# Adjacency masks made on GpSimd instead of VectorE, with one-byte edges moved in pairs, in a two-layer graph attention kernel

## The chip, the cores and the metric

The kernel runs on one core of a Trainium2 chip. Its time is the device time of one execution in microseconds. The core has five engines that run their own instruction streams and meet at semaphores: TensorE (PE, with its weight loads as PEld), VectorE (DVE), ScalarE (ACT), GpSimd (POOL) and SyncE (SP), which here only issues DMAs.

## What is computed

Two graph attention layers over 6144 nodes with 128 features, each with a residual and a layer norm. `adj` is a 6144 x 6144 matrix of int32 zeros and ones (151 MB), and both layers mask with it.

```python
def _L0_gnn_ref(xx_anchor, input, adj, weight):
    anchor_adj = jnp.einsum('md,de,ne->mn', xx_anchor, weight, input)
    scores = jnp.where(adj > 0, anchor_adj, NEG_PAD)
    return jax.nn.softmax(scores / TEMPERATURE, axis=1) @ input

def _L1_gnn_ref(mole_out, adj, W, a1, a2):
    Wh = mole_out @ W
    e = jax.nn.leaky_relu((Wh @ a1)[:, None] + (Wh @ a2)[None, :], negative_slope=0.2)
    att = jax.nn.softmax(jnp.where(adj > 0, e, NEG_INF), axis=1)
    return jax.nn.elu(att @ Wh)

x = _layernorm(x + _L0_gnn_ref(x, L0_gnn_input, adj, L0_gnn_weight), axis=-1)
x = _layernorm(x + _L1_gnn_ref(x, adj, L1_gnn_W, L1_gnn_a1, L1_gnn_a2), axis=-1)
```

## The kernel before

**Layer 0** takes 48 tiles of 128 rows (index t), each in 12 chunks (c) of 512 columns. For each chunk PE makes the scores in three f16 matmuls (lines 462 to 464). DVE adds the mask to them, takes the maximum and writes them to `rows` (L693). After the tile's last chunk DVE makes the bias of the exponential (L752, L756). One tile later ACT exponentiates (L589), PE transposes the result in f32 (L452), ACT copies its high half (L583), DVE makes the low half (L702), and PE multiplies both by `vals` (L428, L430). The end of a tile (scale, residual, layer norm: L720 to L747) is spread over the chunks 3 to 9 of DVE two tiles later. Its reciprocal root is made on POOL (L329), between L744 and L747 of DVE: L747, in chunk 9, waits for it.

**Masks and edges.** SP loads `adj` in four quarters q of 128 x 1536 int32 per tile into `adj_sb`, which holds one tile. DVE turns a quarter into a bf16 mask, 0 or -2^60 (`make_mask`, L670). POOL turns the mask into bf16 edges, 1 or 0 (`make_edges`, L314). SP stores the edges to `edge_rows` in HBM (L250). `neg_mask` and `edges` each hold one tile. So a quarter of the next tile's mask waits for three things: its `adj` has landed, DVE has used the old mask (`masked`), and POOL has turned it to edges (`edges_set`). SP loads a quarter of `adj` once the mask before it is made (`mask_set`, L259); ahead of a tile's loads it waits for PE's transposes L386 and L415 of earlier tiles (L255, L267).

**The first tile** also makes z and `vals`: DVE has z_low (L649), vals_low (L656) and L693 for each chunk, and POOL scales `vals` in four pieces (L306).

**Between the layers** PE makes Wh in 48 matmuls of one node block each (L494), copied out by ACT and DVE.

**Layer 1** takes 12 groups (g) of 512 rows. SP reads the edges back through the transposing DMA, eight parts of six node blocks per group, into four slots of `edgesT`, which lie over the masks (L282). DVE multiplies each of the 48 blocks of edges with the weights (L865, out in eight slots `p1`), and PE accumulates four products of it into PSUM (L523, each f32 matmul being two records in the trace). The group's end is spread over DVE and POOL (L346 to L368). `r_all` holds a factor per row of the group, spread over the partitions by PE (L501) and copied by ACT (L631).

The order of each engine's work is written out by hand: `tile_steps` of each engine and `tile_rstd` of POOL.

Of the kernel before, what the change touches and what calls it, by code (L numbers as in the profile page):

```python
# [31 lines left out]
def build(nc, x, adj, inp, w0, w1, a1, a2, edge_rows, out):  # L32
# [15 lines left out]
    with ExitStack() as ctx:  # L48
# [246 lines left out]
        def _(pool):  # L295
# [13 lines left out]

            def make_edges(t, q):  # L310

                after(pool, edges_out[q], 16 * t)
                pool.wait_ge(mask_set, QUARTERS * t + q + 1)
                nc.gpsimd.tensor_scalar(edges[:, q, :], neg_mask[:, q, :], 1.0 / MASK_BIG, 1.0, ALU.mult,  # L314
                                        ALU.add).then_inc(edges_set, 1)

            for q in range(QUARTERS // 2):
                make_edges(0, q)

            def tile_rstd(t, par, known):  # L320
                ahead = known is None or known < NB - 1
                if scores_of(known):
                    for q in range(QUARTERS // 2, QUARTERS):
                        make_edges(t, q)
# [565 lines left out]
```

## Time and profile before

| | us |
|---|---|
| median of 3 runs (1623.17 to 1624.73) | 1623.41 |
| the profiled execution | 1624.58 |
| its span, first to last instruction | 1622.8 |
| first tile's bias (L756) ends about | 52.9 |
| last tile's bias ends about | 1050.6 |
| first layer 1 weights (L865) start | 1084.8 |

The profiled execution is 1.2 us longer than the median. Layer 0 takes nearly two thirds of the span and layer 1 one third. Busy times are shares of the span, and a busy PE may be a PE whose matmuls wait in line behind each other, so the stages are read one by one. "Idle before, releaser" tells for how long an engine stood still before a line's instructions, and what let it go on.

### The profile page before, as it was taken

Reading aid. Unit: us, or ns where it says so; the run is one execution under the profiler, and the core shown is the slowest. Engines: PE = TensorE matmul, PEld = TensorE weight load, DVE = VectorE, ACT = ScalarE, POOL = GpSimd, SP = SyncE. Lnnn points to the kernel's source line nnn. Section 1 sums busy time; section 2 is a strip of 40 time slices with the busy share of each in tenths; the row PEclk is TensorE's granted clock in tenths of the full one; section 3 lists DMA queues with packets and bytes.
Section 4 is the critical chain, followed back from the end, with each engine's and each line's share of the span. In section 5 each row is a group of like instructions: output and inputs, shape, how many; then the busy total and the mean of one; then the engine's idle time right before and its main releaser. Section 6 shows DMA issues by size and latency. Waiting matters only on the chain.

```text
span 1622.8 us, 36456 instructions
## 1 busy us (share of the span) xinstructions
PE 1583.5 (98%) x13614; PEld 1331.7 (82%) x13614; DVE 1506.9 (93%) x3368; ACT 868.9 (54%) x2111; POOL 431.1 (27%) x330
## 2 busy tenths in 40 slices
PE   6799999999999999999999999989999999999996
PEld 3577777777777777777777777789999999999996
DVE  6999999999999999999999999978999999999996
ACT  3577777777777777777777777881000000000000
POOL 5322323333323232323333232200222222222120
PEclk9899999999999999999999999999999999999998
DMA  7756666666666666666666666447767777767781
GB/s 239 242 181 225 236 239 241 241 240 233 221 224 219 222 222 230 235 241 240 241 238 222 221 220 224 142 83 154 161 145 154 151 151 148 150 144 154 145 163 33
DMA packets 380398, 317.07 MB, mean 195 GB/s; under 512 B 306240, under 2 KB 331072, under 8 KB 380224
## 3 DMA queue, kind: packets, MB, share of 16 engines
q1 hardware_dynamic: 380224, 314.75, 63.6%
q8 instruction: 109, 1.79, 0.4%
q14 instruction: 65, 0.53, 0.1%
HBM read 160.56 MB, written 78.64 MB: 147 GB/s over the span
## 4 chain that ended last, share of the span: by engine, by line
PE 92%; issue 3%; DVE 2%; ACT 1%; POOL 0%; POOLq 0%; DVEq 0%; ACTq 0%
PE ps L523 29%; PE ps L452 15%; PE ps L428 15%; PE ps L430 8%; PE ps L464 7%; PE ps L463 7%; PE ps L462 7%; DVE adj_sb L865 1%; PE ps L494 0%; ACT rows L589 0%; PE ps L415 0%; PE ps L386 0%; ACT pT_hi L583 0%; PE ps L501 0%; PE ps L531 0%
## 5 line engine op out<-in xcount | busy, mean ns | idle before, releaser
L523 PE MATMUL ps<-rows,adj_sb 128*128 128x129 f32 x4608 | 516.7, 275 | 1.4 <-DVE adj_sb L865 1.4
L523 PEld LDWEIGHTS ps<-rows,adj_sb 128*128 128x128 f32 x4608 | 515.6, 192 | 1.6 <-issue 1.6
L865 DVE SCALAR_TENSOR_TENSOR adj_sb<-rows,late,edge_sb 128x512 f32<-128x512 f32 x576 | 440.2, 797 | 44.3 <-PE ps L523 21.2
L428 PE MATMUL ps<-vals,pT_hi 128*128 128x256 f16 x2304 | 442.5, 273 | 0.9 <-ACT att L577 0.8
L583 ACT CAST pT_hi<-ps 128x512 f16<-128x512 f32 x576 | 336.9, 585 | 192.0 <-PE ps L452 181.8
L589 ACT ACTIVATE rows<-rows,exp_bias 128x512 f32<-128x512 f32 x576 | 417.2, 724 | 19.8 <-DVE exp_bias L756 19.8
L693 DVE CUSTOM_DVE_ANT_0 rows<-ps,edge_sb 128x512 f32<-128x512 f32 x576 | 396.3, 688 | 26.0 <-PE ps L464 13.8
L430 PE MATMUL ps<-vals,pT_lo 128*128 128x128 f16 x2304 | 411.7, 219 | 0.0
L314 POOL TENSOR_SCALAR edge_sb<-edge_sb 128x1536 bf16<-128x1536 bf16 x192 | 283.0, 1474 | 470.4 <-DVE edge_sb L670 470.3
L702 DVE TENSOR_TENSOR pT_lo<-ps,pT_hi 128x512 f16<-128x512 f32 x576 | 394.9, 686 | 6.0 <-ACT pT_hi L583 5.8
L452 PE MATMUL ps<-ident,rows 128*128 128x128 f32 x2304 | 349.5, 274 | 2.8 <-DVE pT_lo L702 2.8
L428 PEld LDWEIGHTS ps<-vals,pT_hi 128*128 128x128 f16 x2304 | 225.7, 98 | 87.1 <-DVE pT_lo L702 1.3
L430 PEld LDWEIGHTS ps<-vals,pT_lo 128*128 128x128 f16 x2304 | 225.7, 98 | 66.3 <-issue 0.3
L452 PEld LDWEIGHTS ps<-ident,rows 128*128 128x128 f32 x2304 | 247.3, 141 | 10.1 <-issue 3.7
L628 ACT ACTIVATE zT<-ps,late 128x128 f32<-128x128 f32 x48 | 13.7, 368 | 434.7 <-DVE late L803 434.7
L462 PE MATMUL ps<-zT,xT_hi 128*128 128x512 f16 x576 | 219.4, 381 | 4.4 <-DVE vals L656 4.3
L463 PE MATMUL ps<-zT,xT_hi 128*128 128x512 f16 x576 | 219.3, 381 | 0.0
L464 PE MATMUL ps<-zT,xT_lo 128*128 128x512 f16 x576 | 219.3, 381 | 0.0
L670 DVE TENSOR_SCALAR edge_sb<-adj_sb 128x1536 bf16<-128x1536 int32 x192 | 185.6, 966 | 0.0
L464 PEld LDWEIGHTS ps<-zT,xT_lo 128*128 128x128 f16 x576 | 56.6, 98 | 68.6 <-issue 1.3
L589 ACT ACTIVATION_READ_ACCUMULATOR rows<-rows,exp_bias 128x1 f32 x576 | 109.9, 191 | 0.0
L329 POOL TENSOR_TENSOR small<-small,consts 128x1 f32<-128x1 f32 x48 | 26.4, 550 | 266.5 <-DVE small L744 266.5
(99 smaller groups left out, 737.1 us busy)
## 6 DMA issues: line engine op xcount, KB each, us to landing
adj_sb<-adj SPq DMA_DIRECT2D x192, 768.0 KB, 8.2
edge_rows<-edge_sb SPq DMA_DIRECT2D x192, 384.0 KB, 7.8
rows<-inp SPq DMA_DIRECT2D x4, 768.0 KB, 9.0
xq<-x SPq DMA_DIRECT2D x48, 64.0 KB, 2.0
xr<-x SPq DMA_DIRECT2D x48, 64.0 KB, 1.9
out<-vals SPq DMA_DIRECT2D x12, 256.0 KB, 2.6
edge_sb<-edge_rows SPq DMA_TRANSPOSE x96, 5.6
x1T<-w SPq DMA_DIRECT2D x1, 64.0 KB, 1.9
```

The source lines that it names most:

```text
L428: nc.tensor.matmul(acc, pT_hi[:, s, cols], vals[:, jb, :], start=(jb == 0), stop=False, skip_group_check=True)
L430: mm = nc.tensor.matmul(acc[:, P:2 * P], pT_lo[:, s, cols], vals[:, jb, 0:P], start=False, stop=(jb == NB - 1), skip_group_check=True)
L452: mm = nc.tensor.transpose(ps[:, PT0 + bc % NPT, b * P:(b + 1) * P], rows[:, pb * N + bc * CHUNK + b * P:pb * N + bc * CHUNK + (b + 1) * P ...
L462: nc.tensor.matmul(scores_bank(c), xT_hi[:, par, :], zT[:, 0, cols], start=True, stop=False)
L463: nc.tensor.matmul(scores_bank(c), xT_hi[:, par, :], zT[:, 1, cols], start=False, stop=False)
L464: nc.tensor.matmul(scores_bank(c), xT_lo[:, par, :], zT[:, 0, cols], start=False, stop=True).then_inc(scored, 1)
L523: mm = nc.tensor.matmul(ps[:, 4 * par + k, 0:P + 1], p1_slot(n)[:, k * P:(k + 1) * P], vals1[:, n, 0:P + 1], start=(n == 0), stop=(n == NB ...
L583: nc.scalar.copy(pT_hi[:, bc % PT_SLOTS, :], ps[:, PT0 + bc % NPT, :]).then_inc(pT_hi_set, 1)
L589: nc.scalar.activation(row_chunk(1 - par, c), row_chunk(1 - par, c), ACT.Exp, bias=exp_bias[:, 1 - par:2 - par], scale=EXP_SCALE, accum_ou ...
L693: nc.vector.tensor_tensor_reduce(row_chunk(par, c), scores_bank(c), neg_mask[:, c // QC, w:w + CHUNK], 1.0, -3.0e38, ALU.add, ALU.max, par ...
L702: nc.vector.tensor_tensor(pT_lo[:, s, :], ps[:, PT0 + bc % NPT, :], pT_hi[:, s, :], ALU.subtract).then_inc(pT_lo_set, 1)
L865: nc.vector.scalar_tensor_tensor(out=p1_slot(n), in0=r_all[:, bass.ds(g * CHUNK, CHUNK)], scalar=col_of[:, E_OF, n:n + 1], in1=edgesT[:, p ...
```

## The change

- `make_mask` moves from DVE to POOL, same operation and shape: int32 in, bf16 out. POOL makes mask and edges of a quarter one after the other. In a tile t it makes quarter 3 of this tile and quarters 0 and 1 of the next, then the reciprocal root, then quarter 2 of the next.
- In the first tile POOL makes a mask and its edges after each of the first three pieces of `vals`.
- Edges are kept as one byte each (`edges`, a buffer of its own) and stored as pairs in 16-bit words: half the bytes of each store and of each transposing DMA. `edgesT` gets its slots over the masks alone.
- A transposed pair holds two neighbouring nodes, so DVE reads `edgesT` as bytes with a step of two, and block jb of layer 1 is the even or the odd nodes of 256. The order of Wh's rows (`x1T_pairs`) and of `r_all` follows.

```diff
-        edge_sb = sb("edge_sb", [P, 2, QUARTERS, QW], BF16)
-        neg_mask = edge_sb[:, 0]
-        edges = edge_sb[:, 1]
+        edge_sb = sb("edge_sb", [P, PART_SLOTS * PB * CHUNK // 2], U16)
+        neg_mask = edge_sb[:, 0:N].bitcast(BF16).rearrange("p (q w) -> p q w", w=QW)
+        edges = sb("edges", [P, QUARTERS, QW // 2], U16)
+        edge_bytes = edges[:].bitcast(U8)
...
+        edgesT_bytes = edge_sb[:].bitcast(U8).rearrange("p (s b w h) -> p s b h w", b=PB // 2, w=CHUNK, h=2)
+        x1T_pairs = x1T[:].rearrange("d (u p h) -> d u h p", p=P, h=2)
...
-                sp.dma_start(edge_rows[bass.ds(t * P, P), q * QW:(q + 1) * QW], edges[:, q, :]).then_inc(edges_out[q], 16)
+                sp.dma_start(edge_rows[bass.ds(t * P, P), q * QW // 2:(q + 1) * QW // 2], edges[:, q, :]).then_inc(edges_out[q], 16)
...
+            def make_mask(t, q):
+                pool.wait_ge(adj_in[q], 16 * (t + 1))
+                after(pool, masked, C * (t - 1) + (q + 1) * QC if t > 0 else 0)
+                after(pool, edges_set, QUARTERS * (t - 1) + q + 1 if t > 0 else 0)
+                nc.gpsimd.tensor_scalar(neg_mask[:, q, :], adj_sb[:, q, :], 0.0, -MASK_BIG, ALU.is_le,
+                                        ALU.mult).then_inc(mask_set, 1)
+            def make_edges(t, q):
+                after(pool, edges_out[q], 16 * t)
+                pool.wait_ge(mask_set, QUARTERS * t + q + 1)
+                nc.gpsimd.tensor_scalar(edge_bytes[:, q, :], neg_mask[:, q, :], 1.0 / MASK_BIG, 1.0, ALU.mult,
+                                        ALU.add).then_inc(edges_set, 1)
...
+                if t < NB:
+                    make_mask(t, QUARTERS - 1)
+                    make_edges(t, QUARTERS - 1)
                 if ahead:
-                    make_edges(t + 1, 0)
+                    for q in range(2):
+                        make_mask(t + 1, q)
+                        make_edges(t + 1, q)
                 if ends_tile(known):
                     pool.wait_ge(ve_set, t - 1)
...
                 if ahead:
-                    make_edges(t + 1, 1)
+                    make_mask(t + 1, 2)
+                    make_edges(t + 1, 2)
...
-                nc.tensor.matmul(ps[:, jb % 4, 0:P + 2], x1T[:, jb * P:(jb + 1) * P], w1_wa,
+                nc.tensor.matmul(ps[:, jb % 4, 0:P + 2], x1T_pairs[:, jb // 2, jb % 2, :], w1_wa,
...
-                    if known == 0:
-                        if c in (2, 5, 8):
-                            make_mask(0, c // QC + 1, 0)
-                        elif c >= C - 2:
-                            make_mask(1, c - (C - 2), None)
-                    else:
-                        if c in (0, 2) and scores_of(known):
-                            make_mask(t, 2 + c // 2, known)
-                        if c in (4, 10) and (known is None or known < NB - 1):
-                            make_mask(t + 1, c // 10, None)
...
-                                                       scalar=col_of[:, E_OF, n:n + 1], in1=edgesT[:, part % PART_SLOTS, n % PB, :],
+                                                       scalar=col_of[:, E_OF, n:n + 1], in1=edgesT_bytes[:, part % PART_SLOTS, n % PB // 2, n % 2, :],
```

POOL in a steady tile of layer 0, before, from one reciprocal root to the next (L314 makes edges, L329 the root; in brackets what the instruction waits for):

```order
L329 TENSOR_TENSOR small<-small,consts 128x1 [waits ve_set]
L314 TENSOR_SCALAR edge_sb<-edge_sb 128x1536 [waits mask_set,edges_out1]
L314 TENSOR_SCALAR edge_sb<-edge_sb 128x1536 [waits mask_set,edges_out2]
L314 TENSOR_SCALAR edge_sb<-edge_sb 128x1536 [waits mask_set,edges_out3]
L314 TENSOR_SCALAR edge_sb<-edge_sb 128x1536 [waits mask_set,edges_out0]
L329 TENSOR_TENSOR small<-small,consts 128x1 [waits ve_set]
```

The same stretch of POOL in the changed kernel (L312 makes a mask, L319 edges, L343 the root):

```order
L343 TENSOR_TENSOR small<-small,consts 128x1 [waits ve_set]
L312 TENSOR_SCALAR edge_sb<-adj_sb 128x1536 [waits edges_set,masked,adj_in2]
L319 TENSOR_SCALAR edges<-edge_sb 128x1536 [waits mask_set,edges_out2]
L312 TENSOR_SCALAR edge_sb<-adj_sb 128x1536 [waits edges_set,masked,adj_in3]
L319 TENSOR_SCALAR edges<-edge_sb 128x1536 [waits mask_set,edges_out3]
L312 TENSOR_SCALAR edge_sb<-adj_sb 128x1536 [waits edges_set,masked,adj_in0]
L319 TENSOR_SCALAR edges<-edge_sb 128x1536 [waits mask_set,edges_out0]
L312 TENSOR_SCALAR edge_sb<-adj_sb 128x1536 [waits edges_set,masked,adj_in1]
L319 TENSOR_SCALAR edges<-edge_sb 128x1536 [waits mask_set,edges_out1]
L343 TENSOR_TENSOR small<-small,consts 128x1 [waits ve_set]
```

Four instructions between two roots became eight, and three masks and three edges now stand between this tile's quarter 2 and the next root.

POOL in the first tile before, from the first piece of `vals`:

```order
L306 TENSOR_SCALAR vals<-rows 128x12x128 [waits inp_in0]
L306 TENSOR_SCALAR vals<-rows 128x12x128 [waits inp_in1]
L306 TENSOR_SCALAR vals<-rows 128x12x128 [waits inp_in2]
L306 TENSOR_SCALAR vals<-rows 128x12x128 [waits inp_in3]
L314 TENSOR_SCALAR edge_sb<-edge_sb 128x1536 [waits mask_set] x4
```

And in the changed kernel (L325 is the old L306):

```order
L325 TENSOR_SCALAR vals<-rows 128x12x128 [waits inp_in0]
L312 TENSOR_SCALAR edge_sb<-adj_sb 128x1536 [waits adj_in0]
L319 TENSOR_SCALAR edges<-edge_sb 128x1536 [waits mask_set]
L325 TENSOR_SCALAR vals<-rows 128x12x128 [waits inp_in1]
L312 TENSOR_SCALAR edge_sb<-adj_sb 128x1536 [waits adj_in1]
L319 TENSOR_SCALAR edges<-edge_sb 128x1536 [waits mask_set]
L325 TENSOR_SCALAR vals<-rows 128x12x128 [waits inp_in2]
L312 TENSOR_SCALAR edge_sb<-adj_sb 128x1536 [waits adj_in2]
L319 TENSOR_SCALAR edges<-edge_sb 128x1536 [waits mask_set]
L325 TENSOR_SCALAR vals<-rows 128x12x128 [waits inp_in3]
```

The second to fourth piece of `vals` each moved behind one mask and one edges instruction more.

## Rows read from the trace of the kernel before

**Rows 1.** The page: busy us, share of the span, instructions of each engine.
```profile
PE 1583.5 (98%) x13614; PEld 1331.7 (82%) x13614; DVE 1506.9 (93%) x3368; ACT 868.9 (54%) x2111; POOL 431.1 (27%) x330
```

**Rows 2.** Windows: stretch, length, busy us (instructions) by engine, PE clock, DMA share, GB/s.
```profile
20.00:40.00 20.00, 14.44 (x54) 6.72 (x51) 19.76 (x30) 7.09 (x12) 9.85 (x5) 0.91 0.57 198
40.00:60.00 20.00, 10.29 (x43) 4.52 (x43) 19.79 (x39) 5.92 (x15) 7.85 (x5) 0.83 0.71 237
...
400.00:600.00 200.00, 200.00 (x1718) 153.57 (x1716) 194.17 (x492) 157.22 (x378) 59.62 (x47) 1.00 0.64 233
...
1300.00:1400.00 100.00, 100.00 (x898) 100.00 (x897) 90.11 (x156) 7.56 (x20) 19.36 (x16) 1.00 0.76 150
```

**Rows 3.** Timeline, DVE: start us, length; the bias of tiles 0, 1 and 47.
```profile
52.76 0.15 DVE L756 TENSOR_SCALAR exp_bias<-row_max 128x1 f32<-128x1 f32 x1
...
74.32 0.15 DVE L756 TENSOR_SCALAR exp_bias<-row_max 128x1 f32<-128x1 f32 x1
...
1050.44 0.15 DVE L756 TENSOR_SCALAR exp_bias<-row_max 128x1 f32<-128x1 f32 x1
```

**Rows 4.** Timeline, DVE: the first and the last of the first eight masks.
```profile
14.81 2.61 DVE L670 TENSOR_SCALAR edge_sb<-adj_sb 128x1536 bf16<-128x1536 int32 x1
...
56.23 1.31 DVE L670 TENSOR_SCALAR edge_sb<-adj_sb 128x1536 bf16<-128x1536 int32 x1
```

**Rows 5.** Groups by line: busy us, mean ns of one, idle before them, releaser.
```profile
L670 DVE TENSOR_SCALAR edge_sb<-adj_sb 128x1536 bf16<-128x1536 int32 x192 | 185.6, 966 | 0.0
L314 POOL TENSOR_SCALAR edge_sb<-edge_sb 128x1536 bf16<-128x1536 bf16 x192 | 283.0, 1474 | 470.4 <-DVE edge_sb L670 470.3
L306 POOL TENSOR_SCALAR vals<-rows 128x1536 f16<-128x1536 f32 x4 | 16.5, 4126 | 7.6 <-DMA rows<-inp 7.6
L358 POOL TENSOR_SCALAR zT<-zT 128x512 f32<-128x512 f32 x11 | 20.5, 1863 | 82.0 <-DVE zT L810 82.0
L359 POOL TENSOR_SCALAR zT<-zT 128x512 f32<-128x512 f32 x11 | 23.6, 2144 | 0.0
L348 POOL COPY pT_hi<-x1T 128x512 f32<-128x512 f32 x12 | 7.5, 621 | 45.7 <-PE ps L531 45.7
L329 POOL TENSOR_TENSOR small<-small,consts 128x1 f32<-128x1 f32 x48 | 26.4, 550 | 266.5 <-DVE small L744 266.5
```

**Rows 6.** Timeline, POOL: the first piece of `vals`, then edges in the first tile.
```profile
7.79 4.12 POOL L306 TENSOR_SCALAR vals<-rows 128x1536 f16<-128x1536 f32 x1 [6.03 <-DMA rows<-inp]
...
37.19 1.47 POOL L314 TENSOR_SCALAR edge_sb<-edge_sb 128x1536 bf16<-128x1536 bf16 x1 [6.09 <-DVE edge_sb L670]
```

**Rows 7.** Timeline, DVE: vals_low while POOL works, and alone.
```profile
37.63 1.57 DVE L656 SCALAR_TENSOR_TENSOR vals<-rows,vals 128x512 f16<-128x512 f32 x1
...
42.39 0.68 DVE L656 SCALAR_TENSOR_TENSOR vals<-rows,vals 128x512 f16<-128x512 f32 x1
```

**Rows 8.** Groups by line, DVE: a two-input instruction at a tile's end.
```profile
L731 DVE SCALAR_TENSOR_TENSOR xr<-att,small,xr 128x128 f32<-128x128 f32 x48 | 16.5, 343 | 0.9 <-ACT att L577 0.9
```

**Rows 9.** Timeline, POOL in layer 1: the second waits for the first, the third for the second.
```profile
1227.29 2.15 POOL L359 TENSOR_SCALAR zT<-zT 128x512 f32<-128x512 f32 x1
1229.59 1.52 POOL L362 TENSOR_TENSOR vals<-zT,vals 128x512 f32<-128x512 f32 x1
1231.18 1.59 POOL L366 TENSOR_TENSOR vals<-vals,zT 128x512 f32<-128x512 f32 x1
```

**Rows 10.** Waits of SP's queue: line, waited for, us in total, times, longest.
```profile
SPq L282 <- DVE adj_sb L865: 446.8, 92, 25.8
```

**Rows 11.** Timeline, DVE in layer 1: nine weights in a row without a wait.
```profile
1239.36 6.04 DVE L865 SCALAR_TENSOR_TENSOR adj_sb<-rows,late,edge_sb 128x512 f32<-128x512 f32 x9
```

**Rows 12.** Groups by line: Wh on PE, and two DVE instructions of 512 columns.
```profile
L494 PE MATMUL ps<-late,x1T 128*128 128x130 f32 x96 | 11.4, 277 | 0.1
L693 DVE CUSTOM_DVE_ANT_0 rows<-ps,edge_sb 128x512 f32<-128x512 f32 x576 | 396.3, 688 | 26.0 <-PE ps L464 13.8 <-issue 0.4
L702 DVE TENSOR_TENSOR pT_lo<-ps,pT_hi 128x512 f16<-128x512 f32 x576 | 394.9, 686 | 6.0 <-ACT pT_hi L583 5.8
```

More of the change, by code:

```diff
@@ L27 @@
 F32, F16, BF16 = mybir.dt.float32, mybir.dt.float16, mybir.dt.bfloat16
-I32 = mybir.dt.int32
+I32, U8, U16 = mybir.dt.int32, mybir.dt.uint8, mybir.dt.uint16
 RMAX = bass.bass_isa.ReduceOp.max
@@ L308, in _ @@
                                         SPLIT_SCALE, None, ALU.mult).then_inc(vals_hi, 1)
[L310 to L318, printed above, removed]
+                if q < QUARTERS - 1:
+                    make_mask(0, q)
+                    make_edges(0, q)
             def tile_rstd(t, par, known):
[L321 to L324, printed above, removed]
+                ahead = t < NB - 1
+                if t < NB:
+                    make_mask(t, QUARTERS - 1)
+                    make_edges(t, QUARTERS - 1)
                 if ahead:
-                    make_edges(t + 1, 0)
+                    for q in range(2):
+                        make_mask(t + 1, q)
+                        make_edges(t + 1, q)
                 if ends_tile(known):
@@ L489, in _ @@
                     turn_x1(NB + 1, (NB + 1) % 2, NB + 1)
-                if jb == NB - 1:
+                if jb == NB - 2:
                     pe.wait_ge(x1T_set, NB)
@@ L505, in _ @@
                 for k in range(BPC):
-                    mm = spread_r(col_of[:, R_OF, g * BPC + k:g * BPC + k + 1], ps[:, 4 + g, k * P:(k + 1) * P])
+                    mm = spread_r(col_of[:, R_OF, g * BPC + k:g * BPC + k + 1],
+                                  ps[:, 4 + g, :].rearrange("p (u d h) -> p u h d", d=P, h=2)[:, k // 2, k % 2, :])
                 mm.then_inc(r_turned, 1)
@@ L629, in group_end @@
                 if known is None or known < NG - 1:
-                    nc.scalar.copy(r_all[:, bass.ds((g + 1) * CHUNK, CHUNK)].rearrange("p (k d) -> p k d", d=P),
-                                   ps[:, 4 * (1 - par):4 * (1 - par) + BPC, 3 * P:4 * P]).then_inc(r_spread, 1)
+                    for u in range(2):
+                        bank = 4 * (1 - par) + 2 * u
+                        op = nc.scalar.copy(r_all[:, bass.ds((g + 1) * CHUNK + u * 2 * P, 2 * P)].rearrange("p (d h) -> p h d", h=2),
+                                            ps[:, bank:bank + 2, 3 * P:4 * P])
+                    op.then_inc(r_spread, 1)
                 nc.scalar.copy(x1r_w, ps[:, 4 * (1 - par):4 * (1 - par) + BPC, 2 * P:3 * P]).then_inc(h1_set, 1)
@@ L662, in xT_low @@
                                                in1=xT_hi[:, par, :], op0=ALU.mult, op1=ALU.subtract).then_inc(xT_lo_set, 1)
-            def make_mask(t, q, known):
-                dve.wait_ge(adj_in[q], 16 * (t + 1))
-                after(dve, masked, C * (t - 1) + (q + 1) * QC if known != 0 else 0)
-                after(dve, edges_set, QUARTERS * (t - 1) + q + 1 if known != 0 else 0)
-                nc.vector.tensor_scalar(neg_mask[:, q, :], adj_sb[:, q, :], 0.0, -MASK_BIG, ALU.is_le,
-                                        ALU.mult).then_inc(mask_set, 1)
             xT_low(0, 0)
@@ L885 @@
     out = nc.dram_tensor("out", arrays["x"].shape, F32, kind="ExternalOutput").ap()
-    edge_rows = nc.dram_tensor("edge_rows", arrays["adj"].shape, BF16, kind="Internal").ap()
+    edge_rows = nc.dram_tensor("edge_rows", (arrays["adj"].shape[0], arrays["adj"].shape[1] // 2), U16, kind="Internal").ap()
     build(nc, *aps, edge_rows, out)
```

5 lines of the change are left out of this document (2 added, 3 removed).

## The prediction

> **What bounds the kernel now.** I read the page first: PE is busy 98% of the span, DVE 93%, POOL 27% [rows 1]. Shares over the whole span hide the stages, so next come the windows. In the middle of layer 0 (400 to 600 us) PE is busy throughout, DVE 97%, POOL 30%; in layer 1 (1300 to 1400) PE and its weight loads are busy throughout, DVE 90% [rows 2]. The bias instruction that ends each tile on DVE gives layer 0's pace: over tiles 1 to 47 (1050.44 - 74.32) / 46 = 21.22 us a tile [rows 3]. The reader is to see that DVE, at 97%, is close behind PE but does not set this pace. What is taken off DVE in the steady tiles is therefore worth nothing by itself. Only in the first 60 us is DVE the bound: it is busy 19.8 of 20 us from 20 to 40 and from 40 to 60, while PE is busy 14.4 and 10.3 and is granted a clock of 0.91 and 0.83 [rows 2].
>
> So two questions decide: how much the first tile gains, and whether POOL can carry the masks within 21.2 us a tile.
>
> **What leaves DVE.** 192 masks of 966 ns leave it [rows 5], 3.9 us a tile. In the steady state this is slack (DVE's work goes from 20.6 to 16.7 us a tile) and costs or gives nothing. In the first tile it is on the path that sets the end: there are eight masks up to 57.5 us [rows 4], some of them lengthened by POOL (the first takes 2.61 us), about 10 us together.
>
> **What a mask costs on POOL.** No row shows this operation on POOL (int32 in, compare and multiply). Its bounds are the nearest rows [rows 5]:
> - low: L314, two operations, bf16 to bf16, 1536 columns: 1.47 us. The copy L348, 512 f32 columns in 0.62 us, has the same cost per column once a start of some 0.18 us is taken off.
> - L306, one operation on f32, 1536 columns: 4.1 us. It had no rival: the first ran from 7.79 to 11.91 us [rows 6], when DVE was nearly idle.
> - high: L359, two operations on f32, 512 columns in 2.14 us; three times that is 6.4 us. Part of it is waiting (see the port, below), so this is an outer bound.
>
> POOL thus has two speeds for this kind of instruction, a factor of nearly three apart. L314 alone is fast. It differs from L306, L358 and L359 in two ways: its input is 2 bytes wide, and it is multiply-then-add. The mask has a 4-byte input and is not multiply-then-add, so by either reading it belongs with L306. I take **4.1 us**.
>
> **What edges cost on POOL.** The operation stays multiply-then-add on a bf16 input; only the output becomes a byte. Bounds are 1.47 us (L314) and 4.1 us (L306); I take **1.47 us**, as input and operations are those of L314.
>
> **The port.** In the first tile vals_low (L656) takes 0.68 us alone but 1.57 us when it starts at 37.63, and POOL's edges ran from 37.19 to 38.66 [rows 6, 7]: its end is 38.66 + 0.54, so it stood still until POOL was done. A VectorE instruction with two inputs in SBUF and a POOL instruction take turns. The Trainium skill says this too (SBUF: State Buffer, section "SBUF: two separate sides"): the shared ports are an exclusive lock for a whole instruction. By that rule the trace agrees. In a steady tile L731 and L735 (0.34 us each) [rows 8] are of this kind, and I count L747 with them: POOL waits for them some 0.7 us a tile, and DVE waits up to 4.1 us for each, some 5 us in all, which its 4.5 us of slack just about hold.
>
> **POOL's sum for a tile.** Between two roots stand four masks and four edges (the order's rows): 4 x (4.1 + 1.47) = 22.3. The root is 0.55 [rows 5]. Instructions that wait for the one before start 0.07 to 0.15 us late [rows 9], eight times 0.1 = 0.8. The port 0.7. Sum **24.3 us**, against the 21.2 that PE needs. POOL becomes the bound of layer 0. Behind a late mask stands DVE's L693, behind that PE's scores. Behind the masks stands the root as well, for which L747 in chunk 9 waits, and behind L747 the whole rest of DVE.
>
> **The first two tiles.** POOL starts at 7.79 us: four pieces of vals 16.4, then eight masks and seven edges up to mask 3 of tile 1, 8 x 4.1 + 7 x 1.47 = 43.1, turns with the twelve vals_low 12 x 0.68 = 8.2, gaps 1.6: 77.1. DVE then has three chunks and the bias, about 4.6: 81.7 against 74.3 before, +7.4. The 10 us that DVE is freed of are not seen, since POOL is later than DVE.
>
> **Steady tiles.** 46 x (24.3 - 21.22) = +141.7.
>
> **Layer 1 and what lies between.** I cost these at nothing:
> - The 96 transposing DMAs carry half. SP waits 446.8 us in 92 pieces for DVE to free their slots [rows 10], so the work that hides them is DVE's own; the shorter transfers bring nothing. SP's order of DMAs is unchanged.
> - L865 reads bytes with a step of two. Nine take 6.04 us [rows 11], 0.67 each, and L656 with other types takes 0.68 [rows 7]. PE needs 8 of 898 records per 100 us [rows 2], 0.89 us a block. DVE would have to take 0.08 us more per block before PE waits (10% idle of 0.89). Lower bound nothing, as PE sets the pace; upper bound see the last rival.
> - Wh's weights with a step of two: 96 records, 11.4 us [rows 12]; nothing if the step is free, which I take, as the loads lie beside the products; a doubling would be +11 us. ACT's copy of `r_all` in two parts is ready a group ahead.
>
> **Sum:** 1624.6 + 7.4 + 141.7 = 1773.7 for an execution like the profiled one; the median stood 1.2 us below it: **1772 us**. Without port and gaps POOL's tile is 22.8 us: 46 x 1.6 = 75, hence 1698. If DVE's waits at the port and POOL's wait for L744 add up around the loop (root, chunk 9, nine chunks, L744, root), I put 26 us: 46 x 4.8 + 8 = 229, hence 1852.
>
> **Rival 1, the other side: POOL's mask is fast, too.** If the int32 input or the compare goes at L314's pace, POOL's tile is 4 x 2.95 + 0.55 + 1.5 = 13.8 us and hides under PE. It decides where mask plus edges reach (21.2 - 0.55 - 1.5) / 4 = 4.8 us. What speaks for it: L348 shows that 4-byte input alone is not slow. Against: three rows of tensor_scalar on f32 are slow. Then the gain is the first tile: 10 us less on DVE, less some 2 us, as POOL now works more of the time in which vals_low wants the port: -8, giving 1615.5. A pair between 4 and 4.8 us would leave only 0 to -3.
> The Trainium skill (GPSIMD Engine Reference, section "Elementwise — side-by-side cycle accounting") would have it so: a body of up to two operations is bound by the port at 1.03 cycles per element. An estimate from that page is 1536 x 1.03 / 1.2 GHz = 1.3 us plus a start for the mask, and the whole would come out as in this rival. By that rule L314 and L348 agree; L306 with 4.1 us does not.
>
> **Rival 2: edges slow as well.** If only bf16 on both sides is fast, edges take 4.1 us: 4 x 8.2 + 0.55 + 1.5 = 34.9 us a tile, 46 x 13.7 + 20 = +650, 2270 us. A slow edges instruction with a fast mask would give the forecast's sum again.
>
> **Rival 3: DVE sets layer 1.** If reading bytes cost 0.15 us more per block, 0.07 beyond the slack, 576 x 0.07 = +40 us, with or without the rest. Every row of DVE with 512 columns lies at 0.67 to 0.69 us [rows 7, 11, 12], so I give it little.
>
> **How the numbers follow.** Forecast (POOL bound, 1698 to 1852) 0.55; rival 1 0.30; rival 2 0.13; rival 3 alone 0.02. Rival 1 splits into 0.25 for a gain over 0.2% (3.2 us, about what a measurement of this kernel can tell from no change) and 0.05 for less. Slower 0.55 + 0.13 + 0.02 = 0.70. The range must take in rival 1, since leaving it out would leave out three in ten: 1612 to 1855. The forecast's own range is 1698 to 1852.
>
> **What would show it.** Right: POOL's L312 at about 4.1 us, L319 at 1.5 us, POOL busy near 95% of layer 0, the distance of two biases about 24 us, DVE's L702 and L747 idle behind POOL, layer 1 as long as before. Wrong: L312 at 1.5 us and a distance of 21.2 us; then only the start can have moved. L319 at 4 us means rival 2; L865 over 0.75 us apart means rival 3.

## The result and the profile after

| | before | after |
|---|---|---|
| median of 4 runs, us | 1624.07 (1623.17 to 1625.03) | 2009.69 (2006.08 to 2011.60) |
| span of the profiled execution | 1622.8 | 2006.4 |
| tile 0's bias | 52.76 | 59.77 |
| tile 1's bias | 74.32 | 85.12 |
| tile 47's bias | 1050.44 | 1433.74 |
| first layer 1 weights | 1084.8 | 1468.4 |

The changed kernel takes 1.237 times as long (95% interval 1.236 to 1.239): slower, as forecast, but by 386 us and not by 148, and beyond the stated range of 1612 to 1855. The whole loss stands in layer 0: the last bias comes 383.3 us later, and from the first layer 1 weights to the end of the span it is 538.0 us in both kernels.

The page of the changed kernel, as [rows 1]:

```profile
PE 1681.1 (84%) x13614; PEld 1374.8 (69%) x13614; DVE 1650.3 (82%) x3176; ACT 866.8 (43%) x2121; POOL 1465.0 (73%) x522
```

Windows of the changed kernel, columns as in [rows 2]; the last lies in layer 1:

```profile
400.00:600.00 200.00, 156.70 (x1246) 116.35 (x1245) 162.92 (x331) 113.63 (x274) 193.01 (x63) 0.93 0.38 138
1500.00:1600.00 100.00, 100.00 (x898) 100.00 (x897) 90.48 (x150) 5.61 (x16) 18.70 (x14) 1.00 0.39 78
```

In layer 0 POOL is now busy 96.5% and PE 78%, where it was 30% and 100%. Layer 1 reads as before, apart from the DMA share, which has halved (0.76 to 0.39). DVE does less work (3176 instructions for 3368) and is busy for longer (1650 us for 1507): some of its instructions are lengthened by waiting. The groups by line show which; L312 is the mask, L319 the edges, L343 the root (old L329), L734 and L746 the old L735 and L747, L864 the old L865. They answer to [rows 5, 8]:

```profile
L312 POOL TENSOR_SCALAR edge_sb<-adj_sb 128x1536 bf16<-128x1536 int32 x192 | 1033.1, 5381 | 15.5 <-issue 0.2
L319 POOL TENSOR_SCALAR edges<-edge_sb 128x1536 uint8<-128x1536 bf16 x192 | 282.5, 1472 | 30.0 <-POOL edge_sb L312 22.3 <-DVE part_max L702 7.3
L746 DVE TENSOR_SCALAR xr<-xr,moments,small 128x128 f32<-128x128 f32 x48 | 245.9, 5123 | 57.6 <-POOL small L343 57.6
L734 DVE SCALAR_TENSOR_TENSOR xr<-att,small,xr 128x128 f32<-128x128 f32 x48 | 105.4, 2195 | 0.0
...
L864 DVE SCALAR_TENSOR_TENSOR adj_sb<-rows,late,edge_sb 128x512 f32<-128x512 f32 x576 | 440.2, 797 | 44.3 <-PE ps L539 21.2
```

The mask takes 5.38 us on POOL, not 4.1; the edges take 1.47 us with bytes out. L746 is 0.34 us of work that takes 5.12. The timeline shows both over one tile. POOL (in brackets: idle before, and what ended it):

```profile
794.68 5.38 POOL L312 TENSOR_SCALAR edge_sb<-adj_sb 128x1536 bf16<-128x1536 int32 x1
800.21 1.47 POOL L319 TENSOR_SCALAR edges<-edge_sb 128x1536 uint8<-128x1536 bf16 x1 [0.15 <-DVE part_max L702]
...
815.92 5.38 POOL L312 TENSOR_SCALAR edge_sb<-adj_sb 128x1536 bf16<-128x1536 int32 x1
821.46 1.48 POOL L319 TENSOR_SCALAR edges<-edge_sb 128x1536 uint8<-128x1536 bf16 x1 [0.15 <-POOL edge_sb L312]
823.51 0.56 POOL L343 TENSOR_TENSOR small<-small,consts 128x1 f32<-128x1 f32 x1 [0.57 <-DVE small L743]
824.15 5.38 POOL L312 TENSOR_SCALAR edge_sb<-adj_sb 128x1536 bf16<-128x1536 int32 x1
```

and DVE at the end of the same tile:

```profile
801.35 0.15 DVE L755 TENSOR_SCALAR exp_bias<-row_max 128x1 f32<-128x1 f32 x1
...
816.04 4.09 DVE L730 SCALAR_TENSOR_TENSOR xr<-att,small,xr 128x128 f32<-128x128 f32 x1
...
824.64 4.98 DVE L746 TENSOR_SCALAR xr<-xr,moments,small 128x128 f32<-128x128 f32 x1
830.83 0.15 DVE L755 TENSOR_SCALAR exp_bias<-row_max 128x1 f32<-128x1 f32 x1
```

From one bias to the next it is 29.48 us here. The mean over tiles 2 to 47, (1433.74 - 85.12) / 46 = 29.32, is not that of a steady tile, since two of them stand apart: tile 2 takes 47.23 us and tile 47 22.99. The 44 between take 29.06 on average, and 35 of them 28.97 or 28.98. POOL's own sum is 4 x (5.38 + 0.15 + 1.47 + 0.08) + 0.56 + 0.1 = 29.0. In only 5 of the steady tiles does POOL wait for L743 at its root, 0.57 us each.

Tile 2 is long because the first root comes late. POOL reaches it at 125.00, behind the masks and edges of tile 2's last quarter and of tile 3's first two, and DVE stands still for it:

```profile
125.62 5.51 DVE L746 TENSOR_SCALAR xr<-xr,moments,small 128x128 f32<-128x128 f32 x1 [14.54 <-POOL small L343]
```

That costs 18.2 us once, and the last tile gives 6.1 of them back.

In the tile above L746 waits for nothing that a semaphore shows: its root is done at 824.07, the next mask starts at 824.15, and L746, from 824.64, ends at 829.62, when that mask ends (829.53). It is lengthened, not idle. The waits show who pays for that:

```profile
PE ps L430 <- DVE xr L746: 200.3, 46, 18.0
DVE xr L746 <- POOL small L343: 57.6, 40, 14.5
...
DVE rows L702 <- POOL edge_sb L312: 16.7, 9, 3.0
```

L430 is PE's transpose of the rows that L746 writes, and PE takes its instructions in order: behind it stand the scores and products of the next chunks. DVE waits little for a mask itself (16.7 us in all). PE's clock falls behind that wait, too. From 794.6 to 800.2 PE is busy 1.8 of 5.6 us, and in the next 6.2 us its granted clock is 0.60 of full speed (columns as in [rows 2]):

```profile
800.20:806.40 6.20, 6.20 (x33) 4.44 (x34) 3.01 (x9) 2.96 (x8) 6.11 (x2) 0.60 0.66 203
```

### The profile page after: what moved, and what is told of

Same layout as the page of the kernel before. It is cut to its first block, busy times and chain, and to the rows that moved or that the text cites. A ratio compares the mean times of both kernels' runs of the same rounds, so it can differ in the third digit from the quotient of the medians.

```text
span 2006.4 us, 36466 instructions
## 1 busy us (share of the span) xinstructions
PE 1681.1 (84%) x13614; PEld 1374.8 (69%) x13614; DVE 1650.3 (82%) x3176; ACT 866.8 (43%) x2121; POOL 1465.0 (73%) x522
## 3 DMA queue, kind: packets, MB, share of 16 engines
HBM read 160.56 MB, written 40.89 MB: 100 GB/s over the span
## 4 chain that ended last, share of the span: by engine, by line
PE 43%; POOL 35%; DVE 14%; issue 6%; ACT 1%; POOLq 0%; DMA 0%; DVEq 0%; SPq 0%; ACTq 0%
POOL edge_sb L312 24%; PE ps L539 24%; DVE xr L746 10%; POOL edges L319 8%; PE ps L467 5%; PE ps L443 4%; PE ps L479 2%; PE ps L477 2%; PE ps L478 2%; DVE rows L702 2%; PE ps L445 2%; POOL small L343 1%; DVE pT_lo L711 1%; POOL vals L325 1%; PE ps L430 1%
## 5 line engine op out<-in xcount | busy, mean ns | idle before, releaser
L312 POOL TENSOR_SCALAR edge_sb<-adj_sb 128x1536 bf16<-128x1536 int32 x192 | 1033.1, 5381 | 15.5 <-issue 0.2
L702 DVE CUSTOM_DVE_ANT_0 rows<-ps,edge_sb 128x512 f32<-128x512 f32 x576 | 420.0, 743 | 207.4 <-PE ps L479 186.8
L864 DVE SCALAR_TENSOR_TENSOR adj_sb<-rows,late,edge_sb 128x512 f32<-128x512 f32 x576 | 440.2, 797 | 44.3 <-PE ps L539 21.2
L443 PE MATMUL ps<-vals,pT_hi 128*128 128x256 f16 x2304 | 462.9, 281 | 0.9 <-ACT att L593 0.8
L467 PE MATMUL ps<-ident,rows 128*128 128x128 f32 x2304 | 374.4, 288 | 82.0 <-DVE pT_lo L711 81.9
L445 PE MATMUL ps<-vals,pT_lo 128*128 128x128 f16 x2304 | 428.2, 224 | 0.0
L467 PEld LDWEIGHTS ps<-ident,rows 128*128 128x128 f32 x2304 | 263.6, 148 | 104.0 <-issue 96.8
L319 POOL TENSOR_SCALAR edges<-edge_sb 128x1536 uint8<-128x1536 bf16 x192 | 282.5, 1472 | 30.0 <-POOL edge_sb L312 22.3
L746 DVE TENSOR_SCALAR xr<-xr,moments,small 128x128 f32<-128x128 f32 x48 | 245.9, 5123 | 57.6 <-POOL small L343 57.6
L477 PE MATMUL ps<-zT,xT_hi 128*128 128x512 f16 x576 | 232.1, 403 | 10.0 <-DVE vals L675 10.0
L478 PE MATMUL ps<-zT,xT_hi 128*128 128x512 f16 x576 | 231.4, 402 | 0.0
L430 PE MATMUL ps<-ident,xr 128*128 128x128 f32 x48 | 19.3, 403 | 200.3 <-DVE xr L746 200.3
```

The costliest lines, as they stand in the source:

```text
L312: nc.gpsimd.tensor_scalar(neg_mask[:, q, :], adj_sb[:, q, :], 0.0, -MASK_BIG, ALU.is_le, ALU.mult).then_inc(mask_set, 1)
L319: nc.gpsimd.tensor_scalar(edge_bytes[:, q, :], neg_mask[:, q, :], 1.0 / MASK_BIG, 1.0, ALU.mult, ALU.add).then_inc(edges_set, 1)
L443: nc.tensor.matmul(acc, pT_hi[:, s, cols], vals[:, jb, :], start=(jb == 0), stop=False, skip_group_check=True)
L445: mm = nc.tensor.matmul(acc[:, P:2 * P], pT_lo[:, s, cols], vals[:, jb, 0:P], start=False, stop=(jb == NB - 1), skip_group_check=True)
L467: mm = nc.tensor.transpose(ps[:, PT0 + bc % NPT, b * P:(b + 1) * P], rows[:, pb * N + bc * CHUNK + b * P:pb * N + bc * CHUNK + (b + 1) * P ...
L702: nc.vector.tensor_tensor_reduce(row_chunk(par, c), scores_bank(c), neg_mask[:, c // QC, w:w + CHUNK], 1.0, -3.0e38, ALU.add, ALU.max, par ...
```

## Experiments

Theory A: POOL's price depends on the pair of operations. Theory B: it depends on the width of the input. Beside them stood the question whether the bytes, or DVE's waits at the port, have a part in the loss. All ratios are to the kernel before, in runs on the same chip.

### probe: the instruction by itself

Behind the last work of the kernel before, POOL alone on the core:

```diff
+step(nc.gpsimd.tensor_scalar(dst_b, src_i, 0.0, -MASK_BIG, ALU.is_le, ALU.mult))
+step(nc.gpsimd.tensor_scalar(dst_b, src_i, MASK_BIG, -MASK_BIG, ALU.mult, ALU.add))
+step(nc.gpsimd.tensor_scalar(dst_b, src_f, 0.0, -MASK_BIG, ALU.is_le, ALU.mult))
...
```

> The kernel before with fifteen POOL instructions of 128 x 1536 appended after the last group, when VectorE has no work left, each waiting for the one before, so that each duration is the instruction's own. They vary the input type (int32, f32, bf16), the output type (bf16, f16, f32) and the pair of operations (compare and multiply, multiply and add, multiply and multiply, maximum and add, one operation alone, copy). Theory A, the pair of operations sets the cost: multiply and add take 1.5 us from int32 and from f32 as well, and compare and multiply take over 4 us from bf16 as well. Theory B, the width of the input sets it: everything from int32 and f32 takes 4 us or more, everything from bf16 1.5 us. The mask as it is (int32, compare and multiply) should repeat the 5.38 us of the changed kernel under both; if it takes less, contention made it long.

Timeline of POOL, all 128 x 1536: comparison and multiply on int32 (L388), multiply and add on int32 (L389); comparison and multiply on bf16 (L392), multiply and add on bf16 (L393); maximum and add on f32 (L395); multiply alone on bf16 (L398), multiply and multiply (L400), a copy (L402):

```profile
1619.04 5.41 POOL L388 TENSOR_SCALAR edge_sb<-adj_sb 128x1536 bf16<-128x1536 int32 x1 [1.24 <-DVE vals L877]
1624.53 1.47 POOL L389 TENSOR_SCALAR edge_sb<-adj_sb 128x1536 bf16<-128x1536 int32 x1
...
1633.10 5.38 POOL L392 TENSOR_SCALAR edge_sb<-edge_sb 128x1536 bf16<-128x1536 bf16 x1
1638.56 1.47 POOL L393 TENSOR_SCALAR edge_sb<-edge_sb 128x1536 bf16<-128x1536 bf16 x1
...
1641.67 5.38 POOL L395 TENSOR_SCALAR rows<-adj_sb 128x1536 f32<-128x1536 f32 x1
...
1655.49 4.08 POOL L398 TENSOR_SCALAR edge_sb<-edge_sb 128x1536 bf16<-128x1536 bf16 x1
...
1663.83 1.48 POOL L400 TENSOR_SCALAR edge_sb<-edge_sb 128x1536 bf16<-128x1536 bf16 x1
...
1666.90 1.47 POOL L402 COPY rows<-adj_sb 128x1536 f32<-128x1536 f32 x1
```

Theory A holds and B falls: on every type multiply and add take 1.47 or 1.48 us, comparison and multiply 5.38 to 5.41. The mask as it is takes as long alone (5.41) as in the changed kernel (5.38), so contention did not make it long. An operation alone takes 4.08 to 4.09 (multiply, minimum, comparison): a multiply is cheaper with a second one behind it.

### mult_add and mult_add_again: the fast pair in the changed kernel

`adj` holds only 0 and 1, so adj x 2^60 - 2^60 is the same mask:

```diff
-nc.gpsimd.tensor_scalar(neg_mask[:, q, :], adj_sb[:, q, :], 0.0, -MASK_BIG, ALU.is_le, ALU.mult)
+nc.gpsimd.tensor_scalar(neg_mask[:, q, :], adj_sb[:, q, :], MASK_BIG, -MASK_BIG, ALU.mult, ALU.add)
```

> The changed kernel with one instruction written otherwise: the mask is adj * 2^60 - 2^60 (multiply, add) instead of (adj <= 0) * -2^60; the same values for a matrix of zeros and ones. Theory A (the pair of operations): a mask takes 1.5 us, POOL's tile is 4 x (1.47 + 1.47) + 0.56 and gaps, about 13.5 us, below PE's 21.2, layer 0 is back at 21.2 us a tile, and the time is 1612 to 1624, faster than the kernel before by what the first tile gains (0 to 10 us). Theory B (the width of the input): a mask stays at 4.1 to 5.4 us and the time at 1770 to 2010.

Measured: 1619.35 us, ratio 0.9961 (0.9948 to 0.9974). The same kernel once more:

> The changed kernel with the mask as multiply and add once more, to set it beside the next run on the same chip. As before: 1616 to 1620.

1619.16 us, 0.9963 (0.9951 to 0.9976). Two operation names are worth 390 us of 2010. The window 400 to 600 us of mult_add, and two of its groups:

```profile
400.00:600.00 200.00, 200.00 (x1716) 153.51 (x1715) 175.81 (x454) 157.28 (x378) 117.50 (x86) 1.00 0.52 188
```

```profile
L312 POOL TENSOR_SCALAR edge_sb<-adj_sb 128x1536 bf16<-128x1536 int32 x192 | 283.6, 1477 | 217.8 <-DMA adj_sb<-adj 118.9 <-issue 92.1 <-DVE part_max L702 2.1
L746 DVE TENSOR_SCALAR xr<-xr,moments,small 128x128 f32<-128x128 f32 x48 | 48.3, 1007 | 0.7 <-POOL small L343 0.7
```

PE is the bound again and POOL has 41% left. L746 still waits at the port, but for 0.7 us, and DVE has room. The last bias comes at 1042.46, 8.0 us before [rows 3], nearly all of it from the first tile (its bias at 45.58 for 52.76); of these the median keeps 5.4. In the profiled execution the first layer 1 weights start 7.6 us early (1077.2), yet the span is only 4.7 us shorter, and over the 45 us from there PE's granted clock is 0.92, against 1.00 over the same stretch of before. The profile of the second series (mult_add_again, an execution of 1616.24 us, against 1619.89) bears this out. It starts layer 1 0.7 us earlier and has a clock of 1.00 over its first 45 us, in which PE gets through 395 records for 369. These 26 records, at 100 us for 898, are 2.9 us, and with the 0.7 they are the 3.6 us by which its span is shorter (1614.5 for 1618.1). Why the clock fell in one execution and not in the other is open.

### bytes_only and masks_only: each half of the change alone

bytes_only is the changed kernel with the masks back on DVE, where and when the kernel before made them; masks_only is the kernel before with POOL's and DVE's part of the diff only, the edges left as bf16:

```diff
-                        if c in (0, 2) and scores_of(known):
-                            make_mask(t, 2 + c // 2, known)
...
+                    for q in range(2):
+                        make_mask(t + 1, q)
+                        make_edges(t + 1, q)
```

> The changed kernel with the masks put back on VectorE, in the order of before; edges stay one byte each, in pairs, with layer 1's new row order. If the masks on POOL are all of the loss: 1620 to 1627, no measurable change, since SP's transposes wait for VectorE and not the other way. If bytes cost something in layer 1 (the read with a step of two, the strided weights of Wh): over 1630.

1624.08 us in ten runs, ratio 0.9999 (0.9990 to 1.0009). The bytes bring and cost nothing, while what is written to HBM falls from 78.64 to 40.89 MB. The 576 weights that read bytes take 440.1 us here and 440.2 in the changed kernel.

> The kernel before with only the masks moved to POOL (int32, compare and multiply), edges still bf16. If the masks are all of the loss: 2000 to 2020, as the changed kernel, POOL's tile 29.5 us. If the smaller stores of the byte edges hid a part of the loss in the changed kernel: longer than 2020.

2008.74 us, 1.2368 (1.2347 to 1.2388): the whole loss, with its masks at 5380 ns.

### one_op_mask: the price that was forecast

A mask of one operation costs 4.09 us, the 4.1 of the prediction, and lets its other terms be measured. Its values are not those of the computation.

```diff
-nc.gpsimd.tensor_scalar(neg_mask[:, q, :], adj_sb[:, q, :], 0.0, -MASK_BIG, ALU.is_le, ALU.mult)
+nc.gpsimd.tensor_scalar(neg_mask[:, q, :], adj_sb[:, q, :], 0.0, None, ALU.is_le)
```

> The changed kernel with the mask made by a single comparison (adj <= 0, giving 1 or 0) instead of compare and multiply. The mask's values are then not those of the computation, and the run is read for its time alone. The probe has this instruction at 4.09 us, the duration that the prediction took for a mask. Theory: the sum of the prediction was right and only its term for the mask wrong. POOL's tile is then 4 x (4.09 + 1.47) + 0.56 + gaps of 1.0 to 1.8, 23.8 to 24.7 us, and the time 1750 to 1790 (1772 forecast). Rival: POOL's tile and the time do not follow the mask's duration in proportion (waits at the port or for the root add up differently): outside 1740 to 1800.

1842.07 us, 1.1337 (1.1320 to 1.1355): 70 us over the forecast's sum and outside 1740 to 1800, so the theory falls and its rival stands. No engine is full between 400 and 600 us:

```profile
400.00:600.00 200.00, 172.05 (x1418) 126.74 (x1415) 180.21 (x373) 129.81 (x311) 176.98 (x71) 1.00 0.44 159
```

A tile takes 25.68 us (801.19 to 826.87 on POOL) though POOL's own sum is 23.6. POOL around the root, and DVE beside it:

```profile
801.19 0.57 POOL L343 TENSOR_TENSOR small<-small,consts 128x1 f32<-128x1 f32 x1 [2.04 <-DVE small L743]
801.74 4.09 POOL L312 TENSOR_SCALAR edge_sb<-adj_sb 128x1536 bf16<-128x1536 int32 x1
```

```profile
802.32 3.58 DVE L746 TENSOR_SCALAR xr<-xr,moments,small 128x128 f32<-128x128 f32 x1
...
819.67 2.80 DVE L730 SCALAR_TENSOR_TENSOR xr<-att,small,xr 128x128 f32<-128x128 f32 x1
823.60 1.36 DVE L734 SCALAR_TENSOR_TENSOR xr<-att,small,xr 128x128 f32<-128x128 f32 x1
826.63 0.15 DVE L743 TENSOR_SCALAR small<-moments 128x1 f32<-128x1 f32 x1
```

It is a loop. The root ends and POOL starts the next mask at once; L746, which needs the root, comes 0.6 us later and stands until that mask is done (805.83; it ends at 805.90). PE's transpose L430 waits for L746, twelve chunks follow, L730 and L734 are held by the next masks, so L743 is late, and POOL waits 2.04 us for L743 at its root. DVE's port waits (6.3 us a tile over the means of the three lines) lie on this loop.

### one_op_gate and after_gate: the loop cut

If that is so, it helps to let POOL wait. Where a tile ends, it starts the mask behind the root only when L746 is done:

```diff
                 if ahead:
+                    if ends_tile(known):
+                        pool.wait_ge(x1_set, t - 1)
                     make_mask(t + 1, 2)
                     make_edges(t + 1, 2)
```

> The kernel of one_op_mask (a mask of one comparison, 4.09 us, whose values are not those of the computation), with one wait more on GpSimd: where a tile ends, the mask of the next tile's third quarter starts only when VectorE has written the rows of the tile before the last (the group at L746), which waits for GpSimd's root. If a loop of the root, the rows, TensorE's chunks and the moments set the pace of one_op_mask (25.7 us a tile), the rows fall from 3.8 us behind a mask to about 0.3, GpSimd gives up about 0.7 us, its tile of work (23.6 us) is then the bound, and the tile takes 24.2 us: 47 x 1.5 = 70 us off, 1775 us (1760 to 1800). If the time of one_op_mask comes from something else than where the rows stand (slower instructions on VectorE all along the tile), it stays within 10 us of 1842.

With the wait in the kernel of one_op_mask: 1773.50 us (1771.72 to 1775.37), 1.0921 (1.0903 to 1.0939). 68.6 us off by adding a wait, as the theory of the loop had it (1760 to 1800). POOL, with the same two lines as above, and the group of L748, which is L746 here:

```profile
809.27 0.57 POOL L343 TENSOR_TENSOR small<-small,consts 128x1 f32<-128x1 f32 x1
810.31 4.09 POOL L312 TENSOR_SCALAR edge_sb<-adj_sb 128x1536 bf16<-128x1536 int32 x1 [0.47 <-DVE xr L748]
```

```profile
L748 DVE TENSOR_SCALAR xr<-xr,moments,small 128x128 f32<-128x128 f32 x48 | 16.6, 346 | 112.0 <-POOL small L343 111.9
```

L746 is back at 0.35 us, POOL gives up 0.47 us and no longer waits for L743 in this tile. Its roots lie 24.21 us apart all through the steady tiles (785.06 and 809.27 here), and over 400 to 600 us POOL is busy 94% (188.49 of 200 us).

> The same wait in the changed kernel itself, mask of 5.38 us and all. If its 29.3 us a tile are GpSimd's own work (4 x 5.38 + 4 x 1.47 + the root and the gaps = 28.9) and nothing else, the wait that moves the rows ahead of the mask brings nothing and costs up to 0.7 us a tile: 2005 to 2040. If a loop over VectorE's port waits has a part in it, as in one_op_mask, it gives 0.4 us a tile or more: 1990 or below.

The same wait in the changed kernel: 2021.21 us (2019.04 to 2022.80), 1.2441 (1.2422 to 1.2460), 11.5 us more than the changed kernel and inside the 2005 to 2040 of no gain. The chain of work that ended last, over one tile (start us, us, what; some of the pieces), is now all POOL's, with L748:

```profile
801.20 0.57 POOL small L343
...
801.80 0.36 DVE xr L748
...
802.23 5.39 POOL edge_sb L312
```

From root to root it is 801.20 to 830.59 = 29.39 us. In the changed kernel itself the chain runs from the root over L746 to PE and back to a mask:

```profile
794.03 0.57 POOL small L343
794.63 5.52 DVE xr L746
800.19 0.47 PE ps L430
800.67 0.85 PE ps L467 x4
...
```

So there the loop exists as well, at about the same length (up to 29.48) as POOL's own sum (29.0): cutting one leaves the other. All that POOL waits for L743 in the steady tiles of the changed kernel is 5 times 0.57 us. In the gated kernel the steady tiles take 29.39, POOL's sum and the 0.4 us that it gives up at each root. What sets the steady tile is the 5.38 us mask, and the waits would matter only below it.

### probe2: which pairs are fast

```diff
+step(nc.gpsimd.tensor_scalar(dst_f[:, 0:CHUNK], src_f[:, 0:CHUNK], 0.0, None, ALU.min))
+step(nc.gpsimd.tensor_scalar(dst_f[:, 0:CHUNK], src_f[:, 0:CHUNK], 0.0, -1.0, ALU.max, ALU.add))
+step(nc.gpsimd.tensor_scalar(dst_f[:, 0:CHUNK], src_f[:, 0:CHUNK], 2.0, 1.0, ALU.mult, ALU.add))
+step(nc.gpsimd.tensor_scalar(dst_f, src_f, 1.0, None, ALU.add))
+step(nc.gpsimd.tensor_scalar(dst_f, src_f, 1.0, 2.0, ALU.add, ALU.mult))
+step(nc.gpsimd.tensor_scalar(dst_f, src_f, 1.0, 1.0, ALU.add, ALU.add))
+step(nc.gpsimd.tensor_scalar(dst_f, src_f, 1.0, 2.0, ALU.subtract, ALU.mult))
...
```

> The kernel before, with twelve GpSimd instructions behind its last work, one at a time; the time itself says nothing. 128x512 f32: minimum alone, maximum and add, multiply and add. 128x1536: add alone; add and multiply; add and add; subtract and multiply; multiply and maximum; maximum and multiply; maximum and minimum; equal and multiply (int32 to bf16); a tensor-tensor add. If two operations out of add, subtract and multiply are the one fast kind, those take 1.47 us at 1536 columns, every pair with a maximum, a minimum or a comparison 5.4, and an operation alone 4.1, at a third of it for 512 columns. If what counts is the second operation alone, maximum and multiply is fast and multiply and maximum slow.

```profile
1620.94 1.50 POOL L388 TENSOR_SCALAR rows<-adj_sb 128x512 f32<-128x512 f32 x1 [1.24 <-DVE vals L874]
1622.52 1.93 POOL L389 TENSOR_SCALAR rows<-adj_sb 128x512 f32<-128x512 f32 x1
1624.53 0.62 POOL L390 TENSOR_SCALAR rows<-adj_sb 128x512 f32<-128x512 f32 x1
1625.23 4.10 POOL L391 TENSOR_SCALAR rows<-adj_sb 128x1536 f32<-128x1536 f32 x1
1629.41 1.48 POOL L392 TENSOR_SCALAR rows<-adj_sb 128x1536 f32<-128x1536 f32 x1
1630.97 5.39 POOL L393 TENSOR_SCALAR rows<-adj_sb 128x1536 f32<-128x1536 f32 x1
1636.44 5.41 POOL L394 TENSOR_SCALAR rows<-adj_sb 128x1536 f32<-128x1536 f32 x1
```

In the order of the diff. Half of the expectation falls: two additions take 5.39 us and subtract and multiply 5.41. Of the pairs tried, only add and multiply, multiply and add, and multiply and multiply are fast. Multiply and maximum, maximum and multiply, maximum and minimum, and equal and multiply take 5.37 to 5.40, so the rule is not one of the second operation either.

### vals_only, best and best_bf16: what the fast pair is worth

The upper halves of `vals` (L306) are a single multiply, 4.1 us. A second multiply, by one, should make it fast:

```diff
-                                        SPLIT_SCALE, None, ALU.mult).then_inc(vals_hi, 1)
+                                        SPLIT_SCALE, 1.0, ALU.mult, ALU.mult).then_inc(vals_hi, 1)
```

> The kernel before with one change: the high half of vals on POOL as multiply by 64 and multiply by 1. Masks stay on VectorE, edges stay bf16. vals_low's first two instructions lost 2.4 and 2.6 us behind POOL there, and the first mask 1.6 us. Theory of the port: a gain of 3 to 6 us, 1618 to 1622. Rival (the start is bound by loads): 1623 to 1626.

In the kernel before, alone: 1617.83 us, 0.9963 (0.9950 to 0.9975), 0.2 us below the range of the theory and clear of its rival. The four pieces take 1.67 us on average for 4.13, the twelve vals_low 10.9 us in all for 16.3, and the first bias comes at 45.94 for 52.76.

> The changed kernel with the mask as multiply and add, and with the high half of vals on POOL written as multiply by 64 and multiply by 1 instead of one multiplication (the same values). The probe has one operation at 4.09 us and two multiplications at 1.48. In the first tile of the run with multiply and add, vals_low of VectorE still stands still for some 7.6 us in all behind POOL's four pieces of vals and behind masks. Theory: the port is what makes vals_low wait, for as long as POOL's instruction lasts; then shorter pieces give 2 to 5 us, 1612 to 1617. Rival: VectorE would wait elsewhere in the first tile (for the loads of adj and input, for PE's z): no gain over the run beside it, 1616 to 1620.

In mult_add: 1613.19 us, 0.9929 (0.9916 to 0.9941); the first bias at 40.46, the last at 1037.36. These are mult_add's edit and this one added up: 0.4% and 0.3 to 0.4%.

> The kernel of best (mask as multiply and add on GpSimd, upper values as two multiplications) with two-byte edges, in order, as before the change. If one byte an edge brings nothing in time, as bytes_only says, this stays within 0.2% of best: 1611 to 1616. If the byte edges help once GpSimd and VectorE have room, it is above 1616.

The same without the bytes: 1611.34 us, 0.9920 (0.9905 to 0.9934). The intervals of the two overlap, and both are faster than the kernels before and after; the bytes bring nothing here either.

## Why the prediction was wrong in its size

**What bounds the kernel, and where the loss would fall: right.** PE, not DVE, set the steady tiles, so taking masks off DVE gave them nothing; POOL became the bound, behind it DVE and PE idle; layer 1 and the work between cost nothing (538.0 us both times, Wh's 96 records 12.0 us for 11.4). Rival 3 is out: the mean of L864 (797 ns) is above the 0.75 us that was named as its sign, but the line takes the same 440 us in bytes_only, in the changed kernel and before, and PE is busy throughout; the sign was badly chosen. Edges with bytes out were taken at 1.47 us and took 1.47, so rival 2 is out.

**The step that failed: the mask at 4.1 us.** It took 5.38. The working had three slow rows and one fast, and found two ways in which the fast one differed, width and operations. It then said that by either reading the mask "belongs with L306", and took the price of L306, which has one operation. The mask has two. The row with two operations that are not the fast pair was L359, 2.14 us at 512 columns; the probe gives that pair 1.93 us alone at 512 and 5.38 at 1536. The outer bound of 6.4 came from L359 times three, start and port waits included. With a start of some 0.2 us off it, as was done for L348, L359 gives 0.2 + 3 x 1.9 = 6.0, and nearer the truth than L306. The right price for the steady tiles gives 1772 + 46 x 4 x 1.28 = 2007 us, and with the eight masks of the first two tiles (8 x 1.28 = 10) 2018; 2009.7 was measured. The mask's price is thus nearly all of what was missed, but that the sum comes so near is in part luck, as the other terms below show.

**The range lost that bound.** The mask's price was bounded by 1.47 and 6.4 us, but the upper end of the time, 1852, was worked out with 4.1. With 6.4 it would have been 46 x 4 x 2.3 = 423 us higher. A bound that is written down and not carried into the range bounds nothing. The lower end, 1698, is 1623.4 + 75 and leaves out the +7.4 us of the first two tiles.

**A second step was off, and covered by the first: the port.** "Some 5 us in all, which its 4.5 us of slack just about hold" took DVE's waits for DVE's alone. one_op_mask, with the mask at 4.1 us as forecast, ran at 1842, 70 over the sum, and one_op_gate at 1773.5. What lay above the sum was the loop: 25.7 us a tile, for which the prediction had an upper case of 26 us and 1852 us. With the loop cut a steady tile takes 24.2 us for the 24.3 of the sum, but not by the same terms: no instruction of POOL's is lengthened at the port in the steady tiles (the term of 0.7 us), and 0.47 us of the 24.2 is the added wait. POOL's own work is 23.6 to 23.7. Slack of an engine over a tile does not hold a wait on a loop that passes through another engine. In the changed kernel this cost next to nothing, as after_gate shows, since the dearer mask made POOL's sum as long as the loop.

**The first two tiles: +10.8 for +7.4.** Tile 1's bias came at 85.12 for 81.7. By the mask's price alone it would have been 10 us later than forecast; it was 3.4. The term that was too large is the turns at the port, 12 x 0.68 = 8.2 us for POOL. Between its start and the end of the eighth mask at 80.81, POOL's pieces of `vals` were lengthened by 0.9 us in all and one mask by 0.3. DVE paid for the turns: its twelve vals_low took 26.3 us, 8.2 of it work.

**A term that the sum lacked: the first root.** The prediction says that L747 waits for the root and that the root stands behind the masks, but it charges tile 2 like every other. The tile took 47.23 us and the last one 22.99, together 12 us more than two steady tiles. Against it stand the 7 us of the first two tiles and the steady tile, 29.06 for 24.3 + 4 x 1.28 = 29.42, which is 17 us over 46 tiles. These three together take some 11 us off the 2018, and this is how it comes near the measured time. In one_op_gate they cancel as well (tile 1's bias 6.9 us early, tile 2 11.4 us and the last tile -2.9 us off a steady one), so that its 1773.5 for the forecast's 1772 is luck to that extent.

**Rival 1 had the right mechanism for another operation.** With a fast mask it gave 1615.5 us; mult_add, which has one, took 1619.3, and its last bias was 8.0 us early, as worked out (-8). It was given 0.30, on L348 and on what the Trainium skill states. The Trainium skill (GPSIMD Engine Reference, section "Elementwise — side-by-side cycle accounting") puts a body of up to two operations at 1.03 cycles per element, 1.3 us by an estimate for the mask; the probe's fast pairs and copies agree (1.47), the mask's pair (5.38) and any single operation (4.09) do not, and here the measurement decides.

## What to carry to other kernels

Before work moves to another engine, time that very instruction there, with its operations, not one that resembles it: on GpSimd the same data cost 1.47, 4.09 or 5.38 us by the two operation names, and writing a comparison of 0 and 1 as multiply-and-add turned a loss of 24% into a gain of 0.4%. Where two engines share a port, find the loops through it, and do not set a wait against an engine's average slack. An engine that starts a long instruction just ahead of a short one on the critical path can be better off waiting.

## What the runs showed of the hardware

- GpSimd, tensor_scalar on 128 x 1536, alone on the core: multiply and add, add and multiply, multiply and multiply 1.47 to 1.48 us; one operation alone 4.08 to 4.10; other pairs, two additions among them, 5.37 to 5.41. The types tried (int32, f32, bf16 in, bf16, f16, f32 out) change nothing. From 512 and 1536 columns: (1.48 - 0.62) / 1024 = 0.84 ns a column, (4.10 - 1.50) / 1024 = 2.5, (5.38 - 1.93) / 1024 = 3.4, each with a start of 0.2 us.
- PE's clock: behind 5.6 us in which PE was busy for 1.8, the changed kernel was granted 0.60 over the next 6.2 us, and over the steady part of layer 0 0.93, where the kernel before had 1.00.
- Copies and casts go at the fast pace (1.47), the f32 tensor-tensor add at 2.75 us.
- An f32 tensor_scalar of VectorE with one tensor input (L746, 0.34 us) also stands at the port until GpSimd's instruction is done: 829.62 against 829.53. L730, with two, had ended 1.2 us before the mask that held it did (820.13 against 821.30); why is open.
- A store of one-byte edges in 16-bit words halved the transposing DMAs' bytes and the DMA share of layer 1 (0.76 to 0.39 between 1300 and 1400 us of the kernel before and of bytes_only), with no effect on a time that PE sets.
